# A gated delta-rule recurrence on one core: the first leaf in pieces, a gram split over two waits, reciprocals by way of DRAM, queries moved on GpSimd

## The chip, the cores and the metric

The kernel runs on one core of a Trainium2 chip. The metric is the device time of one execution in microseconds; three runs of the kernel before took 3096.86, 3099.18 and 3108.70 us, median 3099.18. Engines: TensorE (PE), VectorE (DVE), ScalarE (ACT), GpSimd (POOL), and SyncE (SP), which issues the DMAs.

## The reference

One block over x of 2048 tokens and 256 channels: x plus an attention layer, then a feed-forward layer with 8 experts. The change touches the attention's recurrence and its output norm (and a semaphore of the projections). Per head (16 heads of 128):

```python
def step(S, t):
    y = einsum('bhvk,bhk->bhv', S, k_t)
    err = y - v_t
    S = a_t[..., None] * S - (b_t[..., None] * err)[..., None] * k_t[:, :, None, :]
    o = einsum('bhvk,bhk->bhv', S, q_t)
...
mu = mean(o); var = mean(square(o - mu))
o = (o - mu) * rsqrt(var + LN_EPS) * ln_g + ln_b
g = sigmoid(x @ Wg)
return (o * g) @ Wo
```

## The kernel before

Three stages run one after the other: project_inputs (q, k, v, decays a, gates g, all stored to DRAM in scr), recurrence, and feed_forward. All is float32.

The recurrence goes over 32 chunks of 64 tokens (C). A chunk is cut into 16 leaves of 4 tokens (J = 16, R = 4), and all 16 heads are handled together. In a chunk the carried state ST is first applied to the keys and queries of the whole chunk: four "contact" matmul groups of four heads (L1558), each into one PSUM bank, which ACT copies into PQ (contact_copy, L1244). Then come the leaves in order. For leaf j, DVE multiplies the leaf's coefficients in NC by the leaf's right-hand side (L1137), adds up (L1140) to the solution W, and multiplies it by a decay (L1147) into WR, WT or WE. TensorE transposes that (L1723), ACT copies it to WL, TensorE merges it with the masked products of keys ("grams", in BD or OWN) into psM, and leaf j+1 reads psM. A merge after leaf j spans 1, 2, 4 or 8 leaves (merge_of). The gram of the eight-leaf merge after leaf 7 fills two banks, grams 2 and 3 (L1590), masked by ACT (mask_gram_act, L1355), both in the chunk that uses them: after the contacts on TensorE; ahead of leaf 0's WL copy and at leaf 2 on ACT.

At the chunk's end (behind leaf 15) ACT gathers W's last leaves in WE, TensorE transposes WE (L1767), ACT copies that to WTOK, TensorE forms the updates of the state (L1665), DVE adds them (L1087), and the next chunk's contacts follow. GpSimd computes block decays (L816), scales parts of PQ and WT, makes the decayed W (decayed_w, L838 to L843), the decayed queries of the chunk before (decayed_q, into FQ, which is the same memory as SQ) and the output gates (L860).

The output of chunk g-1 is finished inside chunk g, spread over its leaves: squares (ACT, leaf 9), variances (TensorE "var", leaf 10), square root (ACT deviation, L1392, leaf 12), a transpose (TensorE "dev", L1616), a reciprocal on DVE (invert, L1065, leaf 13), eight transposes that broadcast it ("rstd", L1621, leaf 14) and DVE's norm from PSUM (L1070, leaf 15, ahead of the additions to the state). In odd chunks from 3 on the projection by Wo runs too (wo, L1628 and L1688), so that odd and even chunks differ.

The order is written out by hand, leaf by leaf, for every engine (short_jobs and leaf_jobs for TensorE, the chunk functions of the others). Each engine works its own queue in order, with semaphore waits between. TensorE's results go through a ring of five PSUM banks, which a placement computed ahead of time gives out, the longest-held first.

## Time and profile before

| what | value |
|---|---|
| median of three runs | 3099.18 us (3096.86 to 3108.70) |
| span of the profiled execution | 3102.6 us |
| PE / DVE / ACT / POOL busy over the span | 88% / 72% / 52% / 44% |
| projections | 0 to about 620 us |
| recurrence, 32 chunks | about 620 to 2760 us |
| feed-forward | about 2760 us to the end |

The profile is one execution, its span 3.4 us longer than the median. Busy shares tell little for the recurrence, where engines take turns; it is read from the timeline, in which a bracket at the end of a row gives the idle time before it and who ended it.

### The profile page before, as it was taken

What the parts mean: (1) busy time and instruction counts of PE and PEld (TensorE: products, weight loads), DVE (VectorE), ACT (ScalarE), POOL (GpSimd) and SP (SyncE); (2) the same over time, 40 slices, a digit from 0 to 9 for tenths busy, and PEclk for the clock granted to TensorE, in tenths of its full rate; (3) what the DMA queues carried; (4) which work ended last, traced back from release to release, by engine and by line L of the source; (5) the groups of instructions that cost most, each with busy time, mean ns of one, the idle gap of its engine ahead of it and who ended that gap; (6) DMA issues with size and microseconds to landing.
All of it is one profiled execution on the core that took longest, in us unless ns stands there. A gap on an engine that the chain in (4) does not pass through costs nothing. (4 is left out here: it accounts for less than half of the span.)

```text
span 3102.6 us, 48417 instructions
## 1 busy us (share of the span) xinstructions
PE 2732.2 (88%) x14144; PEld 1863.5 (60%) x14144; DVE 2239.8 (72%) x4680; ACT 1610.3 (52%) x3516; POOL 1377.8 (44%) x1760
## 2 busy tenths in 40 slices
PE   7999999768898888988889888898888888859999
PEld 3555555446666666666666666666666666635555
DVE  6777777677888878888788887888887888623332
ACT  6666666545555555555555555555555555412111
POOL 3666676734544445444454444544445444310000
PEclk9999999989999999999999999999999999979999
DMA  3655556533232232322323223232223222034120
GB/s 124 241 225 206 233 230 239 196 82 67 43 57 42 44 65 47 57 42 43 64 49 57 42 44 59 53 57 42 44 51 61 46 53 43 9 107 109 45 38 14
DMA packets 449883, 261.22 MB, mean 84 GB/s; under 512 B 402672, under 2 KB 414672, under 8 KB 447472
## 3 DMA queue, kind: packets, MB, share of 16 engines
q1 hardware_dynamic: 449664, 258.51, 31.5%
q8 instruction: 112, 1.84, 0.3%
q14 instruction: 107, 0.88, 0.1%
HBM read 153.42 MB, written 105.05 MB: 83 GB/s over the span
## 5 line engine op out<-in xcount | busy, mean ns | idle before, releaser
L265 DVE SCALAR_TENSOR_TENSOR A_acc<-A_psY,A_w,A_acc 128x410 f32<-128x410 f32 (+1 forms) x720 | 419.2, 637 | 151.6 <-ACT A_acc L334 151.6
L405 PE MATMUL A_psY<-A_xT,A_w 128*128 128x413 f32 (+1 forms) x960 | 347.2, 510 | 9.1 <-PE A_psAG L411 7.7
L1244 ACT ACTIVATE B_PQ<-B_psM 128x64 f32<-128x64 f32 (+2 forms) x480 | 125.2, 261 | 441.2 <-DVE B_NC L1137 440.9
L1137 DVE TENSOR_TENSOR B_NC<-B_NC,B_psM 128x256 f32<-128x256 f32 x480 | 200.8, 418 | 182.5 <-PE B_psM L1756 92.8
L192 POOL TENSOR_TENSOR A_outs<-A_outs,A_acc 128x410 f32<-128x410 f32 (+1 forms) x240 | 229.7, 987 | 216.1 <-ACT A_outs L342 216.1
L899 POOL TENSOR_TENSOR B_WT<-B_WT,B_G 128x128 f32<-128x128 f32 (+2 forms) x224 | 143.4, 640 | 371.2 <-ACT B_WT L1244 184.3
L1244 ACT ACTIVATE B_WL<-B_psT 64x128 f32<-64x128 f32 (+3 forms) x480 | 148.5, 309 | 265.6 <-PE B_psT L1723 265.4
L405 PEld LDWEIGHTS A_psY<-A_xT,A_w 128*128 128x128 f32 x960 | 180.2, 189 | 165.5 <-issue 164.2
L1140 DVE TENSOR_REDUCE B_W<-B_NC 128x64 f32<-128x320 f32 x512 | 248.7, 486 | 17.6
L334 ACT ACTIVATE A_acc<-A_psY,A_w 128x410 f32<-128x410 f32 (+1 forms) x240 | 166.1, 692 | 162.9 <-PE A_psY L405 161.2
L879 POOL TENSOR_TENSOR B_PQ<-B_PQ,B_G 128x256 f32<-128x256 f32 x128 | 89.4, 699 | 345.5 <-DVE B_WT L1105 345.5
L1756 PE MATMUL B_psM<-B_BD,B_WL 128*128 128x128 f32 x1536 | 228.2, 288 | 12.4 <-ACT B_WL L1244 4.6
L1756 PEld LDWEIGHTS B_psM<-B_BD,B_WL 128*128 128x128 f32 x1536 | 192.5, 192 | 71.9 <-ACT B_WL L1244 69.5
L411 PE MATMUL A_psAG<-A_xT,A_w 128*128 128x410 f32 (+1 forms) x640 | 233.1, 506 | 0.0
L887 POOL TENSOR_TENSOR B_PQ<-B_PQ,B_G 128x256 f32<-128x256 f32 (+1 forms) x192 | 159.6, 845 | 128.3 <-DVE B_WE L1147 127.6
L1023 DVE TENSOR_TENSOR B_NC<-B_NC,B_TMP 128x384 f32<-128x384 f32 (+1 forms) x192 | 184.7, 962 | 3.3
L411 PEld LDWEIGHTS A_psAG<-A_xT,A_w 128*128 128x128 f32 x640 | 120.9, 189 | 99.6 <-issue 99.6
L1568 PE MATMUL B_ring<-B_KQ,B_KL 128*128 128x256 f32 x512 | 139.5, 396 | 25.4 <-DMA B_KQ<-scr 25.3
L1733 PE MATMUL B_psM<-B_OWN,B_WL 64*128 64x128 f32 x448 | 106.7, 319 | 51.7 <-ACT B_WL L1244 51.7
L2048 ACT ACTIVATE C_act_g<-C_psG 128x512 f32<-128x512 f32 (+1 forms) x56 | 33.4, 597 | 228.3 <-PE C_psU L2103 228.3
L1723 PE MATMUL B_psT<-ident,B_WR 128*64 128x128 f32 x256 | 75.7, 296 | 86.3 <-DVE B_WR L1147 85.1
L850 POOL TENSOR_TENSOR B_SQ<-B_PQ,B_E 128x256 f32<-128x256 f32 x128 | 129.4, 1012 | 47.0 <-DVE B_WT L1147 45.6
(207 smaller groups left out, 6588.4 us busy)
## 6 DMA issues: line engine op xcount, KB each, us to landing
B_KQ<-scr SPq DMA_DIRECT2D x96, 512.0 KB, 6.6
scr<-A_outs SPq DMA_DIRECT2D x48, 615.0 KB, 3.5
scr<-A_outag SPq DMA_DIRECT2D x32, 615.0 KB, 5.2
scr<-A_outs SPq DMA_DIRECT2D x48, 409.0 KB, 2.5
A_xc<-nbeta SPq DMA_DIRECT2D x16, 1024.0 KB, 5.9
B_A<-scr SPq DMA_DIRECT2D x32, 512.0 KB, 4.6
B_C<-scr SPq DMA_DIRECT2D x32, 512.0 KB, 6.3
B_G<-scr SPq DMA_DIRECT2D x32, 512.0 KB, 4.6
```

The costliest lines, as they stand in the source:

```text
L192: nc.gpsimd.tensor_tensor(o, o, acc[:, p, n % 2, 0:t1 - t0], ALU.mult).then_inc(silu[p].sem, 1)
L265: nc.vector.scalar_tensor_tensor(a, y, w[:, s, col:col + 1], a, ALU.mult, ALU.add)\
L334: nc.scalar.activation(acc[:, p, n % 2, 0:t1 - t0], psY[p][:, y0:y0 + t1 - t0], ACT.Identity, scale=w[:, s, col + HALO:col + HALO + 1], bi ...
L405: last = nc.tensor.matmul(psY[p][:, y0:y0 + HALO + t1 - t0], wp[:, p, kt, :], xT[:, kt, t0:t1 + HALO], start=kt == 0, stop=kt == KT - 1)
L411: last = nc.tensor.matmul(psAG[p][:, 0:t1 - t0], wp[:, A_ + p, kt, :], xT[:, kt, HALO + t0:HALO + t1], start=kt == 0, stop=kt == KT - 1)
L887: tt(x, x, gl.to_broadcast([128, H, n]), ALU.mult).then_inc(psc.sem, 1)
L899: tt(dst, dst, gr, ALU.mult).then_inc(wsc.sem, 1)
L1023: tt(out, in0, in1, op).then_inc(ncs.sem, 1)
L1137: tt(eq[:, :, :, 1:5], eq[:, :, :, 1:5], left.unsqueeze(2).to_broadcast([128, H, R, R]), ALU.mult)\
L1140: nc.vector.tensor_reduce(W[:, :, lf], eq, AXIS.X, ALU.add).then_inc(ws.sem, 1)
L1244: copy = lambda out, in_: nc.scalar.activation(out, in_, ACT.Copy)
L1756: last = mm(psM[:, 512 * q + rs * i:512 * q + rs * (i + 1)], WL[0:rs, 128 * i:128 * (i + 1)], BD[0:rs, bank, col + rs * part:col + rs * (p ...
```

## The change

- First leaf: DVE multiplies the coefficients by each contact bank straight from PSUM, four heads at a time, and adds up in two halves (first_leaf). ACT's contact copy of a bank waits for DVE's piece of that bank. Later waits on leaf_terms and w_solved are shifted by the added counts.
- Gram 3 of the next chunk is computed at the end of the chunk, one matmul group behind the WE transposes and one behind the updates (next_gram); ACT masks it behind its copy of W's rows. Gram 2 stays behind the contacts, and its mask goes behind leaf 0's WL copy.
- Norm: no dev and rstd transposes. DVE takes the reciprocal in place of the square roots (8 partitions of 128), SyncE stores it to DRAM (rstd_d) and loads it back broadcast to all partitions into FQ, which is SQ; DVE's norm reads that. The square root moves from behind leaf 12 to ahead of leaf 11's WL copy.
- Leaf 15: DVE writes its decayed W straight into WE; ACT's last gather covers leaves 12 to 14.
- GpSimd: decayed_q parts 0 to 2 go later, and wait for the norm of the chunk before instead of the square root; scale_left of leaf 1 goes ahead of them.
- Projections: one semaphore w_used with three counts takes the place of three.

The diff, cut to its core:

```diff
-        -1: [("gram", 2), ("gram", 3)],
+        -1: [("gram", 2)],
...
-        12: ([("gram", 0)] if not last else []) + ([("dev", 0)] if out else []) + ([("wo_rest", 0)] if wo else []),
+        12: ([("gram", 0)] if not last else []) + ([("wo_rest", 0)] if wo else []),
...
-        14: [("ktok", 1)] + ([("rstd", 0)] if out else []) + ([("wo_rest", 1)] if wo else []) + ([("rstd", 1)] if out else []),
+        14: [("ktok", 1)] + ([("wo_rest", 1)] if wo else []),
...
+            def spread_rstd(o):
+
+                wait(sp, rd, o, 1)
+                wait(sp, rld, o, 0)
+                sp.dma_start(rstd_d, sdev[:]).then_inc(rst.sem, 16)
+                wait(sp, rst, o, 1)
+                sp.dma_start(FQ, rstd_d.rearrange("i x -> (i x)").partition_broadcast(128)).then_inc(rld.sem, 16)
...
                 scale_right(g, 1)
                 scale_right(g, 3)
+                past(g, 1)
+                scale_left(g, 1)
                 if g:
                     decayed_q(g - 1, 0)
-                scale_left(g, 1)
-                past(g, 1)
-                if g:
-                    decayed_q(g - 1, 1)
                 past(g, 2)
...
             def invert(o):
-                ps = take_bank(dve, o + 1, "dev", 0)
-                nc.vector.reciprocal(rdev[:], ps[:, 0:8]).then_inc(rd.sem, 1)
+                wait(dve, sd, o, 1)
+                nc.vector.reciprocal(sdev[:], sdev[:]).then_inc(rd.sem, 1)
 
             def norm(o, i):
-                ps = take_bank(dve, o + 1, "rstd", i)
+                wait(dve, rld, o, 1)
                 x = O[:, 8 * i:8 * (i + 1), :]
-                tt(x, x, ps[:].rearrange("p (h c) -> p h c", h=8), ALU.mult).then_inc(on.sem, 1)
+                tt(x, x, SQ[:, 8 * i:8 * (i + 1), :], ALU.mult).then_inc(on.sem, 1)
...
+            def first_leaf(g, eq):
+
+                for n in range(4):
+                    h = slice(4 * n, 4 * n + 4)
+                    left = take_bank(dve, g, "contact", n)[:].rearrange("p (h q t) -> p h q t", h=4, q=2)[:, :, at_p(g), 0:R]
+                    tt(eq[:, h, :, 1:5], eq[:, h, :, 1:5], left.unsqueeze(2).to_broadcast([128, 4, R, R]), ALU.mult)\
+                        .then_inc(ap.sem, 1)
+                    if n == 1:
+                        wait(dve, awm, g - 1, 3)
+                        wait(dve, wxc, g - 1, 1)
+                    if n % 2:
+                        half = slice(8 * (n // 2), 8 * (n // 2) + 8)
+                        wait(dve, ap, g, n + 1)
+                        nc.vector.tensor_reduce(W[:, half, 0:R], eq[:, half], AXIS.X, ALU.add).then_inc(ws.sem, 1)
...
                 for i in range(4):
                     ps = take_bank(act, g, "contact", i)
+                    wait(act, ap, g, i + 1)
...
-                wait(act, wt, g, J)
+                wait(act, wt, g, JM)
                 wait(act, wsc, g, JM // 2)
                 wait(act, wsc0, g, JM // 2 + 1)
-                copy(w_end(12, J), w_leaves(12, J)).then_inc(wec.sem, 1)
+                copy(w_end(12, JM), w_leaves(12, JM)).then_inc(wec.sem, 1)
...
                 w_rows_copy(g)
+                if more:
+                    wait(act, mps, g, 16)
+                    mask_gram_act(g + 1, 3)
...
                     if i % 4 == 3:
                         last.then_inc(wtp.sem, 1)
+                next_gram(g, 0)
                 for i in range(4):
                     run_job(g, ("update", i))
+                next_gram(g, 1)
```

What that does to the queues, in three places. TensorE, from leaf 14 of an odd chunk over its end to the next chunk's leaf 0 (L1595 key tokens, L1621 rstd, L1688 projection, L1767 transposes of WE, L1665 updates, L1558 contacts, L1590 grams 2 and 3), before:

```order
L1595 MATMUL B_ring<-ident,B_KQ 128x128 x4
L1621 MATMUL B_ring<-ident,B_rdev 128x128 x4
L1688 MATMUL B_ring<-B_wo,B_OG 128x256 x4
L1621 MATMUL B_ring<-ident,B_rdev 128x128 x4
L1767 MATMUL B_psM<-ident,B_WE 128x128 x8
L1665 MATMUL B_ring<-B_WTOK,B_KTOK 128x128 x16
L1558 MATMUL B_ring<-B_KQ,B_ST 128x128 x16
L1590 MATMUL B_ring<-B_KQ,B_KC 128x256 x4
L1723 MATMUL B_psT<-ident,B_WR 64x128
```

and in the changed kernel (lines 1626, 1727, 1807, 1687, 1589 and 1621 are the same steps; 1704 is the moved gram):

```order
L1626 MATMUL B_ring<-ident,B_KQ 128x128 x4
L1727 MATMUL B_ring<-B_wo,B_OG 128x256 x4
L1807 MATMUL B_psM<-ident,B_WE 128x128 x8
L1704 MATMUL B_ring<-B_KQ,B_KC 128x256
L1687 MATMUL B_ring<-B_WTOK,B_KTOK 128x128 x16
L1704 MATMUL B_ring<-B_KQ,B_KC 128x256
L1589 MATMUL B_ring<-B_KQ,B_ST 128x128 x16
L1621 MATMUL B_ring<-B_KQ,B_KC 128x256 x2
L1762 MATMUL B_psT<-ident,B_WR 64x128
```

The two rstd bundles are gone, and half of what stood behind the contacts now stands on both sides of the updates.

VectorE, from the additions to the state to the next leaf 0 (L1087 additions, L1023 last step of the leaf solutions, L1137/L1140/L1147 the leaf, L1100 scale_leaf), before:

```order
L1087 TENSOR_TENSOR B_ST<-B_ST,B_ring 128x4x128 [waits B_state_decayed,B_bank3_full]
L1023 TENSOR_TENSOR B_NC<-B_NC,B_TMP 128x128x3 [waits B_leaf_solutions]
L1137 TENSOR_TENSOR B_NC<-B_NC,B_PQ 128x16x4x4 [waits B_decayed_w,B_w_rows_copied,B_contact_copied,B_leaf_solutions]
L1140 TENSOR_REDUCE B_W<-B_NC 128x16x4 [waits B_leaf_terms]
L1147 TENSOR_TENSOR B_WR<-B_W,B_E 128x64 [waits B_w_solved]
L1100 TENSOR_TENSOR B_PQ<-B_PQ,B_E 128x32x4 [waits B_contact_copied]
L1105 TENSOR_TENSOR B_WT<-B_WR,B_E 128x64 [waits B_w_decayed]
```

and in the changed kernel (1101, 1037, then four pieces 1135 and two sums 1143, 1175, 1114):

```order
L1101 TENSOR_TENSOR B_ST<-B_ST,B_ring 128x4x128 [waits B_state_decayed,B_bank2_full]
L1037 TENSOR_TENSOR B_NC<-B_NC,B_TMP 128x128x3 [waits B_leaf_solutions]
L1135 TENSOR_TENSOR B_NC<-B_NC,B_ring 128x4x4x4 [waits B_bank4_full,B_leaf_solutions]
L1135 TENSOR_TENSOR B_NC<-B_NC,B_ring 128x4x4x4 [waits B_bank0_full]
L1143 TENSOR_REDUCE B_W<-B_NC 128x8x4 [waits B_leaf_terms,B_w_rows_copied,B_decayed_w]
L1135 TENSOR_TENSOR B_NC<-B_NC,B_ring 128x4x4x4 [waits B_bank1_full]
L1135 TENSOR_TENSOR B_NC<-B_NC,B_ring 128x4x4x4 [waits B_bank2_full]
L1143 TENSOR_REDUCE B_W<-B_NC 128x8x4 [waits B_leaf_terms]
L1175 TENSOR_TENSOR B_WR<-B_W,B_E 128x64 [waits B_w_solved]
L1114 TENSOR_TENSOR B_PQ<-B_PQ,B_E 128x32x4 [waits B_contact_copied]
L1119 TENSOR_TENSOR B_WT<-B_WR,B_E 128x64 [waits B_w_decayed]
```

The leaf's product no longer waits for the contact copies but for the banks; L1114 still waits for the copies.

VectorE from leaf 13's decay product over the reciprocal and four steps of the leaf solutions to leaf 14's product, before:

```order
L1147 TENSOR_TENSOR B_WT<-B_W,B_E 128x64 [waits B_w_solved]
L1065 RECIPROCAL B_rdev<-B_ring 128x8 [waits B_bank4_full]
L1023 TENSOR_TENSOR B_NC<-B_NC,B_TMP 128x128x3 [waits B_leaf_solutions]
L1023 TENSOR_TENSOR B_NC<-B_X,B_NC 128x128
L1023 TENSOR_TENSOR B_TMP<-B_X,B_NC 128x512 [waits B_leaf_solutions]
L1023 TENSOR_TENSOR B_NC<-B_NC,B_TMP 128x128x2x2 [waits B_leaf_solutions]
L1137 TENSOR_TENSOR B_NC<-B_NC,B_psM 128x16x4x4 [waits B_merge_ps]
```

and in the changed kernel (1175, 1079, 1037, 1162 are the same steps):

```order
L1175 TENSOR_TENSOR B_WT<-B_W,B_E 128x64 [waits B_w_solved]
L1079 RECIPROCAL B_E<-B_E 8x128 [waits B_sdev]
L1037 TENSOR_TENSOR B_NC<-B_NC,B_TMP 128x128x3 [waits B_leaf_solutions]
L1037 TENSOR_TENSOR B_NC<-B_X,B_NC 128x128
L1037 TENSOR_TENSOR B_TMP<-B_X,B_NC 128x512 [waits B_leaf_solutions]
L1037 TENSOR_TENSOR B_NC<-B_NC,B_TMP 128x128x2x2 [waits B_leaf_solutions]
L1162 TENSOR_TENSOR B_NC<-B_NC,B_psM 128x16x4x4 [waits B_merge_ps]
```

The reciprocal keeps its place, reads SBUF instead of a bank, and has 128 elements on 8 partitions instead of 8 on 128.

## Rows read from the trace of the kernel before

**Rows 1.** Busy time of the engines by stage: us, then each engine, clock, DMA.

```profile
900.00:2850.00 1950.00, 1694.50 (x10337) 1241.11 (x10337) 1500.95 (x3310) 1038.80 (x2417) 860.78 (x1162) 0.98 0.27 53
```

**Rows 2.** Timeline of SyncE: start us, us it took to issue; loads of K, KB, Q.

```profile
763.82 4.39 SPq L719 DMA_DIRECT2D B_KQ<-scr  x3
...
1865.27 4.09 SPq L719 DMA_DIRECT2D B_KQ<-scr  x3
...
1994.33 4.54 SPq L719 DMA_DIRECT2D B_KQ<-scr  x3
...
2582.96 4.26 SPq L719 DMA_DIRECT2D B_KQ<-scr  x3
```

**Rows 3.** Timeline, all engines, end of an even chunk and the next leaf 0.

```profile
1864.95 0.27 DVE L1147 TENSOR_TENSOR B_WT<-B_W,B_E 128x64 f32<-128x64 f32 x1
...
1865.82 1.06 PE L1767 MATMUL B_psM<-ident,B_WE 128*128 128x128 f32 x8 [0.62 <-ACT B_WE L1244]
1866.34 1.27 DVE L1070 TENSOR_TENSOR B_O<-B_O,B_ring 128x512 f32<-128x512 f32 x2
...
1866.64 0.40 POOL L816 TENSOR_TENSOR B_G<-B_E 128x128 f32<-128x128 f32 x1 [3.16 <-issue]
...
1868.49 2.48 DVE L1087 TENSOR_TENSOR B_ST<-B_ST,B_ring 128x512 f32<-128x512 f32 x4 [0.88 <-PE B_ring L1665]
...
1873.19 0.84 POOL L843 TENSOR_TENSOR B_WX<-B_A,B_WX 128x256 f32<-128x256 f32 x1
...
1873.72 0.60 ACT L1244 ACTIVATE B_PQ<-B_ring 128x512 f32<-128x512 f32 x1 [0.29 <-PE B_ring L1558]
...
1874.41 0.42 DVE L1137 TENSOR_TENSOR B_NC<-B_NC,B_PQ 128x256 f32<-128x256 f32 x1 [2.65 <-ACT B_PQ L1244]
...
1875.58 0.28 DVE L1100 TENSOR_TENSOR B_PQ<-B_PQ,B_E 128x128 f32<-128x128 f32 x1
```

**Rows 4.** Timeline, TensorE, end of an odd chunk.

```profile
1669.67 1.89 PE L1688 MATMUL B_ring<-B_wo,B_OG 128*128 128x256 f32 x8
...
1671.84 1.04 PE L1767 MATMUL B_psM<-ident,B_WE 128*128 128x128 f32 x8
```

**Rows 5.** Leaf 13 to 14 in the timeline; reciprocals: count, ns min/median/max.

```profile
1664.77 0.42 DVE L1137 TENSOR_TENSOR B_NC<-B_NC,B_psM 128x256 f32<-128x256 f32 x1 [0.16 <-PE B_psM L1756]
...
1859.16 0.71 PE L1756 MATMUL B_psM<-B_BD,B_WL 128*128 128x128 f32 x4
...
1860.97 0.42 DVE L1137 TENSOR_TENSOR B_NC<-B_NC,B_psM 128x256 f32<-128x256 f32 x1
...
L1065 DVE RECIPROCAL B_rdev<-B_ring x32: 198/200/207, 756.9 to 2738.1; 128x8 f32<-128x8 f32 x32
...
L223 DVE RECIPROCAL A_std<-A_std x4: 177/178/178, 14.0 to 26.5; 128x4 f32<-128x4 f32 x4
```

**Rows 6.** A VectorE product beside a busy GpSimd; all products of that line.

```profile
1706.38 1.16 POOL L899 TENSOR_TENSOR B_WT<-B_WT,B_G 128x512 f32<-128x512 f32 x1 [5.76 <-ACT B_WT L1244]
1706.54 1.47 DVE L1023 TENSOR_TENSOR B_TMP<-B_X,B_NC 128x384 f32<-128x384 f32 x1
...
L1023 DVE TENSOR_TENSOR B_TMP<-B_X,B_NC x108: 589/684/1479, 926.9 to 2643.7; 128x512 f32<-128x512 f32 x54, 128x384 f32<-128x384 f32 x54
```

**Rows 7.** Windows of one us: engines as in Rows 1, then TensorE's granted clock.

```profile
1730.00:1731.00 1.00, 0.00 (x0) 0.00 (x0) 0.93 (x4) 0.22 (x1) 0.00 (x0) 1.00 0.00 0
...
1732.00:1733.00 1.00, 0.95 (x3) 0.76 (x4) 1.00 (x2) 0.00 (x0) 0.46 (x1) 0.50 0.00 0
```

**Rows 8.** DMA issues: KB each, median us from issue to landing.

```profile
A_xc<-nbeta SPq DMA_DIRECT2D x16, 1024.0 KB, 5.9
...
att<-B_att SPq DMA_DIRECT2D x16, 128.0 KB, 1.7
```

**Rows 9.** Timeline behind the last chunk: last square root, first norm.

```profile
2737.36 0.36 ACT L1392 ACTIVATE B_E<-B_ring,B_eps 8x128 f32<-8x128 f32 x1 [2.95 <-PE B_ring L1612]
...
2739.62 0.69 DVE L1070 TENSOR_TENSOR B_O<-B_O,B_ring 128x512 f32<-128x512 f32 x1 [1.27 <-PE B_ring L1621]
```

More of the change, by code:

```diff
@@ L458, in chunk_jobs @@
     if g < 0:
-        return [("own", 0, 0), ("own", 0, 1), ("kk", 0, 0), ("kk", 0, 1), ("gram", 0)]
+        return [("own", 0, 0), ("own", 0, 1), ("kk", 0, 0), ("kk", 0, 1), ("gram", 0), ("gram", 3)]
     if g == NCH:
-        return [("qk", n, l) for n in range(3) for l in range(2)] + [("oc", 0), ("oc", 1), ("var", 0), ("dev", 0), ("rstd", 0), ("rstd", 1)]
+        return [("qk", n, l) for n in range(3) for l in range(2)] + [("oc", 0), ("oc", 1), ("var", 0)]
     if g > NCH:
@@ L466, in chunk_jobs, with last_chunk @@
         jobs += [job for job in short_jobs(g, j) + leaf_jobs(g, j) if job[0] not in ("oc_rest", "wo_rest")]
-    return jobs + [("update", i) for i in range(4)]
+    return jobs + [("update", i) for i in range(4)] + ([("gram", 3)] if not last_chunk(g) else [])
+def last_chunk(g):
+    return g + 1 == NCH
 JOBS = [(g, *job) for g in range(-1, NCH + 2) for job in chunk_jobs(g)]
@@ L757, in _ @@
                 loaded(sp, what, NCH - 1)
+            wait(sp, rst, NCH, 0)
+            wait(sp, rld, NCH, 0)
             wait(sp, ldc, NCH, 0)
@@ L1613, in shared_job @@
                                   start=i == 0, stop=i == 7)
-                elif kind == "dev":
-                    wait(pe, sd, g - 1, 1)
-                    last = nc.tensor.transpose(ps[:, 0:8], sdev[:], ident[0:8, 0:8])
-                elif kind == "rstd":
-                    wait(pe, rd, g - 1, 1)
-                    for m in range(4):
-                        i = 4 * n + m
-                        last = nc.tensor.transpose(ps[:, 128 * m:128 * (m + 1)],
-                                                   rdev[:, i:i + 1].to_broadcast([128, 128]), ident[:])
                 elif kind == "wo":
@@ L1667, in updates, with next_gram @@
                             last.then_inc(filled, 1)
+            def next_gram(g, part):
+                if g + 1 == NCH:
+                    return
+                ps, filled = open_bank(pe, g, "gram", 3) if part == 0 else (ring[place[g, "gram", 3][0]], full[place[g, "gram", 3][0]])
+                if part == 0:
+                    loaded(pe, "KB", g + 1)
+                    loaded(pe, "Q", g + 1)
+                    wait(pe, kc, g + 1, 2)
+                (j, i), (bank, col) = [item for item in grams.items() if item[1][0] == 3][part]
+                p, w_, r0 = merge_of(j)
+                hp = 128 // w_
+                left = KC[:].rearrange("p n c -> p (n c)")[:, 256 + 128 * i:][:, 0:128]
+                last = mm(ps[:, col:col + 256], left, KQ[:, (g + 1) % 2, 1:3, i * hp:(i + 1) * hp, r0:r0 + w_], start=True, stop=True)
+                if part:
+                    last.then_inc(filled, 1)
             def run_job(g, job):
```

99 lines of the change are left out of this document (50 added, 49 removed).

## The prediction

> **What bounds the kernel now.** I read the windows by stage first. In the recurrence no engine is full: of 1950 us TensorE (PE) is busy 1694, VectorE (DVE) 1501, ScalarE (ACT) 1039 and GpSimd (POOL) 861 [rows 1]. So it is a chain between engines, and what counts is what ends last at each hand-over. Next, the loads of SyncE show the period, since the load of K, KB and Q goes out once a chunk: an undisturbed pair of chunks takes 1994.33 - 1865.27 = 129.06 us, and the mean pair (2582.96 - 763.82) / 14 = 129.94 [rows 2]. The 0.9 us between the two belong to TensorE's clock, below. There are 15.5 such pairs, so 1 us a pair is 15.5 us, which is just 0.5% of the kernel, about what a measurement of it can tell from no change. Last, I read the timeline where one chunk ends and the next begins, and around leaf 13.
>
> **The change, part by part.** Let 0 be the start of leaf 15's decay product (L1147) at 1864.95.
>
> *The end of a chunk, even chunks* [rows 3]. TensorE's eight transposes (L1767) start at 1865.82, and the row names what they waited for: ACT's copy into WE. That copy waited for L1147. Now DVE writes leaf 15 into WE itself and ACT's copy covers leaves 12 to 14 only, so it stands right behind the copy of key tokens; I take 0.3 us off, not the whole 0.5 that DVE's write alone would allow. The first half of the moved gram lies between the transposes and the updates. A gram bank is four matmuls, about 1 us for two halves, and the halves meet two waits that are each nearly as long; I charge 0.05. So the additions to the state (L1087) and with them the contact banks come 0.25 us earlier. DVE's idle 0.88 us ahead of L1087 covers that.
>
> *The end of a chunk, odd chunks* [rows 4]. Here TensorE is the late one: the key tokens, one rstd bundle, the projection L1688 at 1669.67, another rstd bundle, and L1767 at 1671.84 with no wait. Both bundles go, about 0.4 us each after overlap: -0.8, +0.05 for the gram half, say -0.7.
>
> *The first leaf* [rows 3]. Before, DVE starts at 1874.41, behind the last of ACT's four contact copies (1873.72, 0.60 long). Now DVE takes each contact bank as it fills. A piece of 64 elements costs about 0.21 (the rows' 0.42 for 256 and 0.28 for 128 fall by about 0.14 per 128). Behind the last piece ACT still copies its bank, and scale_leaf (L1100) waits for it: 1873.72 + 0.21 + 0.60 + hand-overs = 1874.63 against 1875.58 now, 0.95 earlier. That is the most this part can give, if nothing else holds L1100 or L1147. The mask of gram 2 goes behind the WL copy, where ACT has room; gram 3's mask falls into ACT's wait for the first contact bank.
>
> *What may hold them.* The norms (L1070 at 1866.34, two of 0.68) read PSUM today. After the change both of their inputs lie in SBUF. The trace shows what such a product does beside a busy GpSimd: at 1706.54 one took 1.47 us where its least is 0.59, and it got going when the GpSimd product of 1706.38 ended [rows 6]. The same hold works the other way round. GpSimd's block_decays start at 1866.64, 0.3 us behind the first norm, and its products end at 1874.03 (1873.19 + 0.84). If the norms push that back by their remaining 0.9 us, the last one ends at 1874.9, at 1875.1 with L1147 between. L1147 and L1100 at the first leaf read SBUF twice as well, and would want the port at 1874.1 to 1874.4. Then L1100 starts at about 1875.0, not 1874.4 (1874.63 less the 0.25). By this an even chunk gains 0.6 in all instead of 1.2, an odd one about 0.8 instead of 1.6: 1.4 us a pair with the hold and 2.8 without it. I take 1.4, since [rows 6] is the same kind of product.
>
> The Trainium skill has a rule on this (SBUF — State Buffer, section "SBUF: two separate sides"): the port pair that VectorE and GpSimd share is "an exclusive lock", held for a whole instruction, by a VectorE product with two SBUF inputs too. By that rule the gain is the 1.4; without it, it would be 2.8; the trace agrees with the rule at 1706.54.
>
> *Reciprocals at leaf 13.* A reciprocal of 4 elements a partition takes 0.178 us and one of 8 takes 0.200 [rows 5]. The new one has 128. Products grow by 0.14 us from 128 to 256 elements, 1.1 ns an element [rows 3]; at that rate it would take 0.33. The slope between its own two rows (0.022 / 4 = 5.5 ns an element) gives 0.20 + 120 x 0.0055 = 0.86. These rows are the same instruction, so I take 0.86, i.e. 0.66 more, and keep 0.13 more as the other end. None of it is covered in an even chunk: leaf 14's product starts at 1860.97 without idle time, while the matmul that it needs had begun at 1859.16 and took 0.71. In an odd chunk the same product waited 0.16 for TensorE (1664.77), which covers as much now that the dev transpose is gone from its queue. Cost: 2 x 0.66 - 0.16 = 1.2 us a pair (0.1 at the other end).
>
> The Trainium skill says that the pipe divides with "a repeat count of 8" (VectorE: DVE Perf Modes, section "First, the fixed hardware budget"). Taken as eight cycles an element that would be an estimate of 1.2 us for the instruction, and 0.7 us a pair more than I charge, 3117 in all; no row here has so many elements.
>
> *The way through DRAM.* After the reciprocal, SyncE writes 4 KB, waits, and issues a broadcast of 512 KB. A store lands in 1.7 us; the nearest broadcast is 1024 KB in 5.9 [rows 8], so half of it I put at 4.3. Leaf 13's decay product ends at about 1858.4, the reciprocal at 1859.3, the store lands at 1861.2, the broadcast at about 1866, against a norm that wants it at 1866.34 + 0.66 = 1867.0. It is hidden by 1 us in even chunks and by more in odd ones. On SyncE only the att store and the next K, KB, Q load queue behind it, and they wait for leaf 15 anyway. At the end of the recurrence nothing hides it: from the square root (2737.36, 0.36) to the first norm it was 2739.62 [rows 9]; now 1 + 2 + 4.3 = about 7.3 behind 2737.7: 5 us once.
>
> *The rest.* GpSimd's later queries keep their number and lie before anyone asks for them; the deviation's earlier place on ACT is one where ACT waits for transposes; one semaphore for three in the projections removes no work. Nothing.
>
> *TensorE's clock.* At 1730 to 1731 TensorE does nothing, and from 1732 its granted clock is 0.50, the lower of its two levels, 1.2 GHz instead of 2.4 [rows 7]. This gap between leaf 13's and leaf 14's work is in every even chunk, and the longer reciprocal widens it from 1.5 to 2.2 us; where the rstd bundles stood, TensorE now idles another 1.2 us. Falls cost 0.9 us a pair today. I put them at 1.2 after (+0.3); the bounds are 0 and +1.4 (a fall in every even chunk, at the chunk's end where TensorE is on the chain).
>
> *Sum per pair:* -1.4 + 1.2 + 0.3 = +0.1 us, times 15.5 = +1.6; with the end +5: about +7. The span goes from 3102.6 to 3109.5, and as the profiled span lies 3.4 us above the median of 3099.2, I predict **3106 us**.
>
> **The rivals.** (1) *One of the two prices is not paid.* If the reciprocal runs at one element a cycle, or if the hold on the port does not reach the first leaf, 1.1 or 1.4 us a pair come back: 3106 - 20 = 3086, on the edge of what counts as faster. For it: two rows with 4 and 8 elements, 0.02 us apart, are little to draw a slope from, and the hold depends on tenths of a microsecond. (2) *Neither is paid:* 3106 - 15.5 x 2.5 = 3067. (3) *The clock (slower).* If the widened gap takes the clock down in every even chunk, the transposes, the gram half and the updates run at 1.2 GHz on the chain: +1.1 us a pair above my 0.3: 3106 + 17 = 3123. It decides when two falls in three chunks become the rule. For it: no work fills the gap; against: today most even chunks pass with 1.5 us. (4) *The broadcast is late (slower).* If it lands over 7.7 us after the reciprocal in even chunks, both norms and the state's additions behind them on DVE wait; 1.5 us late costs, less the cover of 0.9, 0.6 us in an even chunk and nothing in an odd one, +9: 3115; with KQ's load in its way twice that. That the gram's new place does nothing is no rival: without it TensorE would still be busy when the first leaf's transpose comes.
>
> **How the numbers follow.** Forecast 0.33; (1) 0.22, half of it past the line at 3083.7; (2) 0.17; (3) 0.18; (4) 0.10. Faster by over 0.5%: 0.11 + 0.17 = 0.28. Slower by over 0.5% (above 3114.7): 0.28. Within: 0.33 + 0.11 = 0.44. The likeliest case's own range is 3098 to 3114. The range of 3062 to 3132 takes in (2) and (3).
>
> **What would show it.** A reciprocal row near 0.9 us (or 0.3); L1147 and L1100 of leaf 0 longer than 0.27 and 0.29; GpSimd's last product ending near 1874.9 on this scale; L1767 0.3 and 0.7 us behind where I put it or not; the norm waiting for a DMA or not; the mean pair at 130.0 and the count of clock falls. The forecast is wrong if DVE is not what starts leaf 14, or if a ring bank or a load turns up as a new wait.

## The result, and the profile after

The changed kernel takes **3112.31 us** (median of 6 runs, 3106.33 to 3115.26) against 3098.75 (6 runs) for the kernel before: a ratio of 1.0038, 95% interval 1.0024 to 1.0052. It is slower by a small amount that this measurement can just see, and within the half per cent that the prediction called no change. The profiled execution has a span of 3112.4 us, 9.8 more than that of before.

The period hardly moved. The loads of K, KB and Q in the timeline of SyncE (start us, us it took to issue):

```profile
759.24 4.27 SPq L720 DMA_DIRECT2D B_KQ<-scr  x3
...
1733.48 4.02 SPq L720 DMA_DIRECT2D B_KQ<-scr  x3
...
1863.18 4.32 SPq L720 DMA_DIRECT2D B_KQ<-scr  x3
...
2581.79 5.57 SPq L720 DMA_DIRECT2D B_KQ<-scr  x3
```

The mean pair is (2581.79 - 759.24) / 14 = 130.18 us (129.94 before [rows 2], forecast 130.0); the pair between the second row and the third is 129.70. Under this calm lie large moves. First the same product, leaf 13, leaf 14 and then leaf 0 of an even chunk, and leaf 15 and leaf 0 around an odd chunk's end, in the timeline of the kernel **before**:

```profile
1858.14 0.27 DVE L1147 TENSOR_TENSOR B_WT<-B_W,B_E 128x64 f32<-128x64 f32 x1
...
1861.94 0.27 DVE L1147 TENSOR_TENSOR B_WR<-B_W,B_E 128x64 f32<-128x64 f32 x1
...
1875.39 0.27 DVE L1147 TENSOR_TENSOR B_WR<-B_W,B_E 128x64 f32<-128x64 f32 x1
...
1930.07 0.27 DVE L1147 TENSOR_TENSOR B_WT<-B_W,B_E 128x64 f32<-128x64 f32 x1
...
1941.48 0.27 DVE L1147 TENSOR_TENSOR B_WR<-B_W,B_E 128x64 f32<-128x64 f32 x1
```

Its leaf 15 in the even chunk is at 1864.95 [rows 3], so leaf 15 to the next leaf 0 took 10.44 us there, 11.41 in the odd one, and leaf 13 to 14 3.80. (L1147 is L1175 now, L1767 is L1807, L1100 is L1114, L1070 is L1084.) **After**, an even chunk's end, all engines:

```profile
1855.38 0.27 DVE L1175 TENSOR_TENSOR B_WT<-B_W,B_E 128x64 f32<-128x64 f32 x1
...
1859.86 0.27 DVE L1175 TENSOR_TENSOR B_WR<-B_W,B_E 128x64 f32<-128x64 f32 x1
...
1862.86 0.27 DVE L1175 TENSOR_TENSOR B_WE<-B_W,B_E 128x64 f32<-128x64 f32 x1
...
1863.61 1.67 PE L1807 MATMUL B_psM<-ident,B_WE 128*128 128x128 f32 x8 [1.37 <-ACT B_WE L1272]
...
1866.07 2.64 PE L1687 MATMUL B_ring<-B_WTOK,B_KTOK 64*128 64x128 f32 x32
...
1869.23 3.81 PE L1589 MATMUL B_ring<-B_KQ,B_ST 128*128 128x128 f32 x32
...
1873.69 0.27 DVE L1175 TENSOR_TENSOR B_WR<-B_W,B_E 128x64 f32<-128x64 f32 x1
```

Leaf 13 to 14 is 4.48; leaf 15 to leaf 0 is 10.83, longer than before. The way from the first contact matmul (L1589) to leaf 0's product is 4.46, where it was 5.51; but from the transposes (L1807) to L1589 it is 5.62, where it was 4.06 (before, the contact matmuls start at 1869.88). The eight transposes take 1.67 us (1.06 in rows 3). The windows say why (engines as in rows 1, then the granted clock):

```profile
1858.00:1860.00 2.00, 0.43 (x4) 0.19 (x2) 1.90 (x5) 0.22 (x1) 0.00 (x0) 1.00 0.60 215
...
1864.00:1865.00 1.00, 1.00 (x7) 1.00 (x6) 1.00 (x3) 0.53 (x1) 0.45 (x1) 0.50 0.37 87
```

Between 1858 and 1860 TensorE has 0.43 us of work, later it stands 1.37 us before L1807, and while the eight transposes run, the granted clock goes to 0.50, 1.2 GHz. It was below 0.9 over this stretch at all 14 ends of the even chunks 2 to 28 (the first chunk is 0), against 5 of 14 before. An **odd** chunk's end has full clock:

```profile
1928.90 0.27 DVE L1175 TENSOR_TENSOR B_WE<-B_W,B_E 128x64 f32<-128x64 f32 x1
...
1929.89 1.04 PE L1807 MATMUL B_psM<-ident,B_WE 128*128 128x128 f32 x8
...
1933.93 3.81 PE L1589 MATMUL B_ring<-B_KQ,B_ST 128*128 128x128 f32 x32
...
1938.38 0.27 DVE L1175 TENSOR_TENSOR B_WR<-B_W,B_E 128x64 f32<-128x64 f32 x1
1938.46 0.91 POOL L857 TENSOR_TENSOR B_WX<-B_A,B_WX 128x256 f32<-128x256 f32 x1
...
1938.72 0.80 DVE L1114 TENSOR_TENSOR B_PQ<-B_PQ,B_E 128x128 f32<-128x128 f32 x1
...
1941.55 0.27 DVE L1175 TENSOR_TENSOR B_WT<-B_W,B_E 128x64 f32<-128x64 f32 x1
```

Leaf 15 to leaf 0 is 9.48 us, 1.93 less. At leaf 0 the scaling L1114 takes 0.80 us instead of 0.29: it ends right behind GpSimd's L857, at 1939.37. It reads 0.79 or 0.80 behind 14 of 14 odd chunks and 0.29 behind every even one, and leaf 0 to leaf 1 is 3.17 instead of 2.54. The pieces L1135, one of whose inputs is in PSUM, keep their 0.22 us beside GpSimd's products.

The reciprocal (count, ns min/median/max), the broadcast (KB, us from issue to landing), and the end of the recurrence:

```profile
L1079 DVE RECIPROCAL B_E<-B_E x32: 933/933/941, 751.6 to 2736.4; 8x128 f32<-8x128 f32 x32
```

```profile
B_SQ<-rstd SPq DMA_DIRECT2D x32, 512.0 KB, 3.5
```

```profile
2735.97 0.36 ACT L1421 ACTIVATE B_E<-B_ring,B_eps 8x128 f32<-8x128 f32 x1 [2.82 <-PE B_ring L1643]
2736.36 0.94 DVE L1079 RECIPROCAL B_E<-B_E 8x128 f32<-8x128 f32 x1 [16.30 <-ACT B_E L1421]
2737.32 0.29 SPq L736 DMA_DIRECT2D rstd<-B_E  x1
2738.54 0.34 SPq L738 DMA_DIRECT2D B_SQ<-rstd  x1
2741.96 1.29 DVE L1084 TENSOR_TENSOR B_O<-B_O,B_SQ 128x512 f32<-128x512 f32 x2 [4.67 <-DMA B_SQ<-rstd]
```

From the last square root to the first norm it is 5.99 us, for 2.26 before [rows 9].

**Where the 9.8 us are.** I cut the two spans at the same places: leaf 15 of the first chunk, leaf 15 of the last chunk but one, and the last store of the attention output.

| stretch | before | after | difference |
|---|---|---|---|
| start to leaf 15 of chunk 0 | 697.76 | 694.17 | -3.6 |
| 30 chunks | 1947.96 | 1948.86 | +0.9 |
| last chunk and output | 109.14 | 114.02 | +4.9 |
| last store to the end of the span (feed-forward) | 347.74 | 355.35 | +7.6 |

The first row says nothing of the change: leaf 15 of chunk 0 comes at 693.3 to 698.9 in the fourteen profiles of this study, with the changed grams at 694.2 in one kernel and at 698.3 in another. The last row is code that the change does not touch. In the fourteen profiles it takes 347.7 to 355.4 us, and one kernel, profiled twice, gave 348.3 and 351.1. So most of the difference between the two profiled spans is no effect of an edit, or at least none that is shown.

### The profile page after: what moved, and what is told of

It reads as the page before. It is cut to its first block and busy times, and to the rows that moved or that the text cites. A ratio compares the mean times of both kernels' runs of the same rounds, so it can differ in the third digit from the quotient of the medians.

```text
span 3112.4 us, 48158 instructions
## 1 busy us (share of the span) xinstructions
PE 2729.2 (88%) x13856; PEld 1849.1 (59%) x13856; DVE 2288.6 (74%) x4808; ACT 1611.5 (52%) x3516; POOL 1392.2 (45%) x1760
## 5 line engine op out<-in xcount | busy, mean ns | idle before, releaser
L1165 DVE TENSOR_REDUCE B_W<-B_NC 128x64 f32<-128x320 f32 x480 | 233.2, 486 | 16.5
```

Of the source, the lines that this page charges most:

```text
L1165: nc.vector.tensor_reduce(W[:, :, lf], eq, AXIS.X, ALU.add).then_inc(ws.sem, 1)
```

## The experiments

All ratios are to the kernel before, run beside it on the same chip (medians of 3096.9 to 3099.1 us). The table counts the even chunk ends at which TensorE's granted clock was below 0.9 while the last transposes and the first updates ran, and gives the mean pair in the profiled execution by leaf 15 of chunks 1 and 29 (before 129.78, after 130.06 by this measure). Both come from one execution of each kernel. The mean granted clock of the whole program is on record for every execution and points the same way: 0.974 to 0.981 for the kernel before, 0.961 to 0.964 for the changed one, 0.961 to 0.963 for norm_only, 0.969 to 0.972 for short_recip and filler2, 0.974 to 0.978 for filler3, 0.978 to 0.982 for bank_order in its two runs, and 0.982 to 0.984 for bank_filler.

| kernel | median us | ratio, 95% | ends at half clock | mean pair |
|---|---|---|---|---|
| old_norm | 3095.23 | 0.9989 (0.9976 to 1.0003) | 0 of 14 | 129.51 |
| norm_only | 3134.54 | 1.0119 (1.0103 to 1.0136) | 14 | 132.01 |
| filler | 3101.67 | 1.0013 (1.0001 to 1.0024) | 4 | 129.72 |
| short_recip | 3074.05 | 0.9924 (0.9907 to 0.9940) | 12 | 128.30 |
| bank_order | 3063.96 | 0.9888 (0.9871 to 0.9904) | 5 | 127.59 |
| first_only | 3100.15 | 1.0004 (0.9994 to 1.0014) | 1 | 129.62 |
| gram_only | 3129.49 | 1.0093 (1.0076 to 1.0110) | 8 | 131.40 |
| filler2 | 3100.29 | 1.0007 (0.9994 to 1.0020) | 12 | 129.70 |
| filler3 | 3087.12 | 0.9960 (0.9948 to 0.9972) | 7 | 128.66 |
| bank_early_q | 3065.35 | 0.9885 (0.9865 to 0.9904) | 4 | 127.39 |
| bank_filler | 3060.60 | 0.9873 (0.9855 to 0.9892) | 0 | 127.08 |
| bank_order_again | 3062.95 | 0.9882 (0.9864 to 0.9901) | 5 | 127.42 |

### old_norm: the change without its new normalization

```diff
-        14: [("ktok", 1)] + ([("wo_rest", 1)] if wo else []),
+        14: [("ktok", 1)] + ([("rstd", 0)] if out else []) + ([("wo_rest", 1)] if wo else []) + ([("rstd", 1)] if out else []),
...
-                nc.vector.reciprocal(sdev[:], sdev[:]).then_inc(rd.sem, 1)
+                ps = take_bank(dve, o + 1, "dev", 0)
+                nc.vector.reciprocal(rdev[:], ps[:, 0:8]).then_inc(rd.sem, 1)
...
-            spread_rstd(NCH - 1)
```

> The changed kernel with the normalization path of the kernel before: deviation after leaf 12, one transpose of the deviations at leaf 12, a reciprocal of 128x8, eight broadcasting transposes at leaf 14, no store and no broadcast through DRAM; pieces at the first leaf, gram split and the later queries stay. The theory (the chunk boundary gained what the trace of the changed kernel shows, and the new normalization path took it back in three parts: VectorE's longer reciprocal 0.68 and 0.42 us in an even and an odd chunk, TensorE's clock 1.57 us at the even chunk's end and 0.3 at leaf 12, and 3.4 us in the epilogue) expects leaf 13 to leaf 14 at 3.8 and 4.07 us, full clock at the even chunk's end, from the last scaling of a chunk to the first of the next 9.3 us (even) and 9.5 (odd), a pair of chunks at 126.7 where undisturbed, and some 3055 to 3065 us. The rival in which the clock falls come from the shorter boundary itself expects the reciprocal and the epilogue back alone: a pair at 128.6 and about 3090 us. The rival in which the boundary's gain is an artefact of where the time is cut expects 3098, the kernel before.

Measured 3095 us: both the theory's 3055 to 3065 and the first rival's 3090 missed. The second rival's 3098, the kernel before, is nearest, but its reason, that the boundary's gain is an artefact, is not the one: contact to leaf 0 kept its gain (4.46 us for 5.51). The reciprocal's time came back (leaf 13 to 14 at 3.80 and 4.07) and so did the clock, but an even boundary was 10.38 us, not 9.3, and an odd one 11.56. The timeline of an even end, and under it the line of the waits from 900 to 2650 us, in which 27 chunks end (us in total, times, longest):

```profile
1861.12 1.06 PE L1801 MATMUL B_psM<-ident,B_WE 128*128 128x128 f32 x8 [0.50 <-ACT B_WE L1257]
...
1863.08 0.70 PE L1698 MATMUL B_ring<-B_KQ,B_KC 128*128 128x256 f32 x2 [0.90 <-DVE B_O L1069]
...
1863.71 2.06 PE L1681 MATMUL B_ring<-B_WTOK,B_KTOK 64*128 64x128 f32 x32
...
PE B_ring L1698 <- DVE B_O L1069: 23.2, 27, 1.0
```

The moved gram (L1698) stands 0.90 us behind VectorE's normalization. That is no dependence of data. By the placement in the kernel's own code the gram's bank in the ring was that of the second half of the broadcast reciprocals, and these are read until the normalization ends. So the new normalization path does something that the diff doesn't say: it takes the one tenant out of the ring that the moved gram would have to wait for.

### norm_only: the new normalization alone, on the kernel before

```diff
-                ps = take_bank(dve, o + 1, "dev", 0)
-                nc.vector.reciprocal(rdev[:], ps[:, 0:8]).then_inc(rd.sem, 1)
+                wait(dve, sd, o, 1)
+                nc.vector.reciprocal(sdev[:], sdev[:]).then_inc(rd.sem, 1)
...
+                sp.dma_start(rstd_d, sdev[:]).then_inc(rst.sem, 16)
+                wait(sp, rst, o, 1)
+                sp.dma_start(FQ, rstd_d.rearrange("i x -> (i x)").partition_broadcast(128)).then_inc(rld.sem, 16)
```

> The kernel before with the normalization through DRAM alone (deviation at leaf 11, reciprocal of 8x128, store, broadcast, no transposes of it on TensorE). The theory expects leaf 13 to 14 at 4.5 us in both kinds of chunk (3.80 and 4.07 before), TensorE at half clock at the end of most even chunks, a pair at about 131 to 132 us (129.06 undisturbed before, plus 1.1 for the reciprocal and up to 1.9 for the clock), the epilogue 3.4 us longer, and 3125 to 3135 us in all. The rival (the clock falls come from the shorter boundary and not from the missing transposes) expects a pair at 130.2 to 130.9 with as many falls as before, and 3116 to 3119 us.

3134.54 us and a mean pair of 132.01: as the theory said. Timeline of TensorE at an even end:

```profile
1880.09 1.91 PE L1764 MATMUL B_psM<-ident,B_WE 128*128 128x128 f32 x8 [1.49 <-ACT B_WE L1251]
...
1882.03 2.76 PE L1662 MATMUL B_ring<-B_WTOK,B_KTOK 64*128 64x128 f32 x32
```

The transposes take 1.91 us for 1.06, the updates 2.76 for 2.06. With the first leaf and the grams as before, 14 of 14 even ends run at half clock: it is not the shorter boundary that lowers the clock. It is what left TensorE's queue, or the longer reciprocal; short_recip tells these two apart. (The kernel also has the single semaphore of the projections, ahead of the recurrence.)

The total holds something that the theory did not name. Behind an odd chunk the transposes come 0.87 us earlier, but contact to leaf 0 takes 6.19 us for 5.51:

```profile
1956.26 0.84 POOL L850 TENSOR_TENSOR B_WX<-B_A,B_WX 128x256 f32<-128x256 f32 x1
...
1956.29 1.10 DVE L1144 TENSOR_TENSOR B_NC<-B_NC,B_PQ 128x256 f32<-128x256 f32 x1 [2.54 <-ACT B_PQ L1251]
```

Leaf 0's product takes 1.10 us for 0.42 beside GpSimd's last product. It is the hold that the prediction priced, here on the product itself.

### short_recip: the reciprocal cut short

```diff
-                nc.vector.reciprocal(sdev[:], sdev[:]).then_inc(rd.sem, 1)
+                nc.vector.reciprocal(sdev[:, 0:8], sdev[:, 0:8]).then_inc(rd.sem, 1)
```

> The changed kernel with the reciprocal cut to the first 8 of 128 columns; the other columns stay deviations, so the normalization is left out for most rows. It prices VectorE's reciprocal alone. The theory expects leaf 13 to 14 at 3.80 and 4.07 us again, so 1.1 us less in a pair, 0.7 less in the epilogue, and about 3094 us, with TensorE still at half clock at the even chunk's end, since its work is as small as before. The rival (the longer wait of TensorE for the reciprocal is what lowers the clock) expects the clock back too: another 1.9 us in a pair, and about 3066 us.

```profile
L1079 DVE RECIPROCAL B_E<-B_E x32: 182/182/191, 750.0 to 2705.2; 8x8 f32<-8x8 f32 x32
```

182 ns for 933, and 3074.05 us: 20 under the theory's 3094 and 8 over the rival's 3066, so both missed. Leaf 13 to 14 fell to 3.78 and 3.80 us in the mean, 0.7 in both kinds of chunk and not 0.7 and 0.4: the 4.07 of the odd chunk before was not VectorE's, so my 1.1 was too small as a bound and 1.4 is what the instruction costs in the changed kernel. 12 of 14 even ends kept half clock, against the rival, which is why it isn't 3066; together with norm_only this leaves the work that left TensorE's queue as the main cause of the falls. The other 16 us of the 38 under the changed kernel lie in fewer or shorter clock falls elsewhere (mean pair 128.30, where 1.4 less gives 128.66), in the epilogue (114.02 to 110.73 us) and in the feed-forward part; I didn't separate them.

### first_only and gram_only: one half of the boundary each, on the kernel before

```diff
+                    tt(eq[:, h, :, 1:5], eq[:, h, :, 1:5], left.unsqueeze(2).to_broadcast([128, 4, R, R]), ALU.mult)\
+                        .then_inc(ap.sem, 1)
...
+                        first_leaf(g, eq)
...
```

> The kernel before with the first leaf in pieces alone: grams, normalization and the order of the queries stay. The theory expects from the first contact matmul to the first scaled W of a chunk 4.45 us for 5.51, nothing else changed, so 2.1 us less in a pair (127 undisturbed), and 3063 to 3068 us. The rival (the gain of the changed kernel's boundary needs the gram out of the way) expects less than 0.4 us per chunk and 3085 or more.

```diff
+                next_gram(g, 0)
                 for i in range(4):
                     run_job(g, ("update", i))
+                next_gram(g, 1)
...
```

> The kernel before with the eight-leaf gram split into TensorE's two waits at the chunk's end, and the last W written straight into its place; first leaf, normalization and order of the queries stay. The theory expects no gain at the first leaf (5.5 us from contact to W), and TensorE waiting about 1 us per chunk at the moved gram for the bank that the broadcast reciprocals hold until VectorE has normalized: a pair at 131 us and 3120 to 3130 us. The rival (taking the gram from behind the contact matmuls is worth something by itself, since leaf 0's second product follows sooner) expects 0.3 to 0.6 us per chunk back, and 3100 to 3115.

The pieces alone changed nothing (3100.15, forecast 3063 to 3068: a miss), though the way from contact to leaf 0's W did fall from 5.51 to 4.46. The timeline shows where it went:

```profile
1871.25 1.89 PE L1604 MATMUL B_ring<-B_KQ,B_KC 128*128 128x256 f32 x8
...
1872.06 0.27 DVE L1160 TENSOR_TENSOR B_WR<-B_W,B_E 128x64 f32<-128x64 f32 x1
...
1872.98 0.27 PE L1737 MATMUL B_psT<-ident,B_WR 128*64 128x128 f32 x1
...
1874.79 0.97 POOL L852 TENSOR_TENSOR B_SQ<-B_PQ,B_E 128x256 f32<-128x256 f32 x1
...
1875.22 0.66 DVE L1160 TENSOR_TENSOR B_WT<-B_W,B_E 128x64 f32<-128x64 f32 x1
```

Eight gram matmuls, 1.89 us, begin behind the contact matmuls at 1871.25, and leaf 0's transpose (L1737) comes 0.92 us behind its W at 1872.06; leaf 0 to leaf 1 is 3.15 for 2.54. Then leaf 1's decay product takes 0.66 us for 0.27 beside GpSimd's query product of 1874.79, and leaf 1 to 2 is 2.91 for 2.52. The gain of 1.06 is handed back in two steps within two leaves.

The gram split alone costs 0.9%, as the theory said (3129.49 us, forecast 3120 to 3130). Its waits from 900 to 2650 us have the line of old_norm again:

```profile
PE B_ring L1692 <- DVE B_O L1075: 17.9, 19, 1.1
```

So neither half pays alone as it was tried. The pieces need the gram out of the way, and the gram needs a bank that is free. What the gram split would give alone with a free bank was not run.

### bank_order: the free bank by one line

```diff
-    return jobs + [("update", i) for i in range(4)] + ([("gram", 3)] if not last_chunk(g) else [])
+    return jobs + [("update", 0), ("update", 1)] + ([("gram", 3)] if not last_chunk(g) else []) + [("update", 2), ("update", 3)]
```

This is old_norm with the banks dealt out in another order.

> The kernel with the pieces, the gram split, the later queries and the normalization of before, with one line more: in the list that deals out the five banks of the ring, the moved gram stands between the second and the third update and not behind the fourth, so its bank is the one that the key tokens held and not the one of the second half of the broadcast reciprocals. In the trace with that list unchanged TensorE stands 0.9 to 1.0 us at the moved gram behind VectorE's normalization, in every chunk, which makes the way from the chunk's last transposes to the first update 2.6 us for 1.5. The theory (that wait is the whole reason why the old normalization gained nothing) expects 1.5 us there, a pair of chunks at 127.1 us, and 3052 to 3062 us. The rival in which the wait comes back at the next bank (the second updates, which now hold the reciprocals' banks) expects 0.5 us of it at each chunk and 3070; the rival in which TensorE's clock falls at the even chunk's end, as in the changed kernel, expects another 1.6 us per pair and 3080.

> The kernel with pieces, split gram in the key tokens' bank, the old normalization and later queries once more, beside the three above, for its interval and for the change from chip to chip. The theory expects 3060 to 3066 us and a ratio of 0.987 to 0.991; were the gain of the first run chance, the ratio would be above 0.993.

3063.96 us, 2 us above the theory's 3052 to 3062, and 3062.95 in the second run, inside its range: **1.2% faster than the kernel before**, 1.6% faster than the changed one. The wait line at the moved gram is gone, transposes to first update are 1.5 us at full clock, and the rival's wait at the second updates isn't there. The changed kernel frees the same bank, and pays for it with a store, a broadcast, a longer reciprocal and the clock.

### bank_early_q: do the later queries matter?

```diff
-                past(g, 1)
-                scale_left(g, 1)
                 if g:
                     decayed_q(g - 1, 0)
+                scale_left(g, 1)
+                past(g, 1)
...
```

> The kernel with pieces, split gram in the key tokens' bank and the old normalization, and now GpSimd's three query products in the order of before. In the run with the pieces alone VectorE's scaling at leaf 1 took 0.66 us for 0.27, with a query product of GpSimd running beside it, and the way from leaf 1 to leaf 2 was 2.91 us for 2.52. The theory (the later queries pay only through this) expects 2.52 to 2.91 us there, thus 0 to 0.8 us more per pair, and 3064 to 3076 us. The rival (GpSimd's order matters for what waits for the queries, and the early order was better) expects 3055 to 3062.

3065.35 us, no difference from bank_order, and leaf 1 to 2 at 2.52 us. So the early queries alone do not slow the decay product of leaf 1; in first_only a late leaf 1 came with them, and whether that alone is enough no run shows. The later queries are worth nothing here.

### filler, filler2, filler3, bank_filler: idle work for TensorE

```diff
+FILL = {11: (("gram", 0), 8), 13: (("decay", 2), 8), 14: (("ktok", 1), 8)}
...
+                    if g % 2 == 0 and g + 1 < NCH and j in FILL:
+                        ps = open_bank(pe, g, *FILL[j][0])[0]
+                        for m in range(FILL[j][1]):
+                            nc.tensor.transpose(ps[:, 128 * (m % 4):128 * (m % 4 + 1)], ident[:], ident[:])
```

> The changed kernel with idle work for TensorE in even chunks: eight transposes of the identity more at each of leaves 11, 13 and 14, into the bank that the next job opens, where the trace shows TensorE waiting for VectorE; nothing is computed with them. If missing work on TensorE is what lowers its clock at the even chunk's end, the clock stays at full there, the boundary of an even chunk comes to 9.3 us (10.83 in the changed kernel), leaf 12 to 13 to 2.96, a pair to 127.7 to 128.0 and the kernel to about 3083 us. If the clock falls for another reason, or the transposes stand in the way, it stays at 3112 or rises by up to 1.8 us per pair, to 3140.

Mean pair 129.72, not 128: a miss, and the trace of ScalarE and TensorE tells why:

```profile
1473.32 0.60 ACT L1273 ACTIVATE B_KTOK<-B_ring 128x512 f32<-128x512 f32 x1 [1.65 <-PE B_ring L1627]
...
1473.81 0.35 ACT L1273 ACTIVATE B_WE<-B_WT 128x192 f32<-128x192 f32 x1
...
1474.42 1.07 PE L1812 MATMUL B_psM<-ident,B_WE 128*128 128x128 f32 x8 [1.14 <-ACT B_WE L1273]
```

Idle work ahead of the key tokens made their copy late (1473.32), ScalarE's copy into WE stands behind it, and the transposes come 2.08 us behind leaf 15 in the mean of the 14 even ends for 0.84. The time, 3101.67 us, misses 3083 too. The clock was kept at 10 of 14 ends, and the time spent on the way. filler2 drops the entry for leaf 14:

> The changed kernel with eight idle transposes at each of leaves 11 and 13 of the even chunks, and none at leaf 14, where in the run with three such places the key tokens came 1.2 us later and ScalarE's copy of the last W terms stood behind their copy (last scaling to last transposes 2.13 us for 0.85). The theory expects that delay gone (0.75), and the clock at full at leaf 12 and in most chunk ends, since the idle time just ahead of the first fall and of the second is filled: a pair at 128 us and about 3083 us. The rival (the idle time at leaf 14 alone is enough to lower the clock at the chunk's end) expects full clock at leaf 12 alone, 0.3 us less in a pair than in the changed kernel, and 3105.

Mean pair 129.70, 12 of 14 ends at half clock; leaf 12 to 13 fell from 3.18 to 2.96 in the mean. The rival holds: with leaves 11 and 13 filled, idle time at leaf 14 is still enough. The time of 3100.29 is near the rival's 3105. filler3 keeps leaves 11 and 13 and puts eight transposes behind the key tokens:

```diff
+                if g % 2 == 0 and g + 1 < NCH:
+                    ps = open_bank(pe, g, "update", 0)[0]
+                    for m in range(8):
+                        nc.tensor.transpose(ps[:, 128 * (m % 4):128 * (m % 4 + 1)], ident[:], ident[:])
```

> The changed kernel with idle transposes of TensorE in even chunks: eight at leaf 11, eight at leaf 13, and eight behind the key tokens of leaf 14, into the bank that the first update opens next, so that nothing on ScalarE comes later. The run with idle work at leaves 11 and 13 alone left the fall at the chunk's end; the run with idle work ahead of the key tokens took most of it away and delayed the last transposes by 1.3 us. The theory (the fall at the even chunk's end follows from TensorE's idle time at leaf 14 and its wait there) expects the last transposes 0.75 us behind the last scaling, 1.5 us from there to the first update and 4.05 to the first contact matmul, 9.3 us for the boundary (10.95 in the changed kernel), a pair at 128.2 and about 3080 to 3088 us. If the clock still falls there, the time stays within 5 us of the run with two places, 3100.

3087.12 us: work that computes nothing makes the changed kernel 0.8% faster, and faster than the kernel before. An even end that kept its clock:

```profile
1853.41 1.04 PE L1809 MATMUL B_ring<-ident 128*128 128x128 f32 x8
...
1854.20 0.27 DVE L1176 TENSOR_TENSOR B_WE<-B_W,B_E 128x64 f32<-128x64 f32 x1
...
1854.95 1.06 PE L1816 MATMUL B_psM<-ident,B_WE 128*128 128x128 f32 x8 [0.50 <-ACT B_WE L1273]
...
1856.46 2.06 PE L1688 MATMUL B_ring<-B_WTOK,B_KTOK 64*128 64x128 f32 x32
...
1863.47 0.52 DVE L1176 TENSOR_TENSOR B_WR<-B_W,B_E 128x64 f32<-128x64 f32 x1
```

Leaf 15 to leaf 0 is 9.27 us, for 10.83. Half of the ends still fall, so it isn't all that could be had. The last row is worth a look: with TensorE at full speed the even chunk reaches leaf 0 early enough to meet GpSimd's last product (1863.02, 0.85 long), and the decay product takes 0.52 us for 0.27.

> The kernel with pieces, split gram in the key tokens' bank, the old normalization and later queries, plus eight idle transposes at leaves 11 and 13 of even chunks. Its trace without them shows half clock at the end of some even chunks (last transposes to first update 1.86 us in the mean for 1.5, to the first contact matmul 4.42 for 4.05). If idle time at these leaves lowers the clock, the mean pair comes from 127.6 to 127.1 us and the kernel to about 3056 us; if not, it stays at 3064, and if the idle work is in the way, it rises to 3070.

```profile
1838.46 0.27 DVE L1161 TENSOR_TENSOR B_WE<-B_W,B_E 128x64 f32<-128x64 f32 x1
...
1839.21 1.06 PE L1806 MATMUL B_psM<-ident,B_WE 128*128 128x128 f32 x8 [0.50 <-ACT B_WE L1258]
...
1840.11 0.60 PE L1699 MATMUL B_ring<-B_KQ,B_KC 128*128 128x256 f32 x2
...
1840.72 2.06 PE L1682 MATMUL B_ring<-B_WTOK,B_KTOK 64*128 64x128 f32 x32
...
1847.73 0.27 DVE L1161 TENSOR_TENSOR B_WR<-B_W,B_E 128x64 f32<-128x64 f32 x1
```

3060.60 us for the 3056 expected, none of the 14 even ends at half clock, mean pair 127.08 where 127.1 was expected. The price of the clock is gone from these ends. Against bank_order it is 3 us, which the intervals do not tell apart; the profile does, and the mean granted clock of the four executions (0.982 to 0.984 for 0.978 to 0.982).

## Why the prediction was right, and where it wasn't

The time came out at 3112.3 for 3106, within half a per cent of before as forecast; the working held only in part: two terms were off by about 1 us a pair, in opposite directions, so that the time hits is in good part luck. Per pair of chunks, typical pairs at full clock:

| term | forecast | measured | from |
|---|---|---|---|
| transposes L1807 earlier, even / odd | -0.3 / -0.7 | -0.12 / -0.87 | 0.87 to 0.75; 1.86 to 0.99 behind leaf 15 |
| first leaf in pieces, a chunk | -0.95 | -1.06 | 5.51 to 4.45 from contact |
| leaf 0 to 1, even / odd | (hold) | +0.12 / +0.63 | 2.54 to 2.66 / 3.17 |
| chunk's end, sum | -1.4 | -2.4 | -1.06 even, -1.30 odd |
| reciprocal | +1.2 | +1.1 | 0.68 even, 0.42 odd |
| clock | +0.3 | +1.5 | the rest of 130.18 - 129.94; L1807 to L1589 alone: mean 5.71 for 4.30 in even chunks |
| sum | +0.1 | +0.24 | |

- **The chunk's end.** The step that failed is the price of the hold between VectorE and GpSimd at leaf 0. I took 1.4 us a pair for it; it is 0.5, in the odd chunk alone. The mechanism is there (L1114 at 0.80 ends with L857), and it is the rule of the Trainium skill that the prediction cited (SBUF — State Buffer, section "SBUF: two separate sides"), which the trace agrees with. The norms push GpSimd's products back too, by less than the 0.9 us that I took: behind even chunks the last of them ends 9.10 us behind leaf 15 in the kernel before and 9.64 in the changed one; over the study it is 9.08 to 9.12 wherever the norms read PSUM and 9.62 to 9.67 wherever they read SBUF. The larger error was whom that meets. In the even chunk the slow clock makes leaf 0 so late, at 10.83, that GpSimd is through. filler3, where the clock is back at half of the ends, shows the hold there too, at 0.25 us in the row shown and at 0.24 to 0.52 in 5 of 14 ends. In bank_order, with leaf 0 at the same 9.27 us behind leaf 15 but with norms from PSUM, it is absent.
- **The reciprocal.** 933 ns, forecast 860 from the slope between two short rows; the slope from 8 to 128 elements is (933 - 182) / 120 = 6.3 ns. 0.16 us of cover in the odd chunk was 0.26. Right. The estimate of 1.2 us that I worked out from the Trainium skill (VectorE: DVE Perf Modes, section "First, the fixed hardware budget") was 0.3 us too long; no row here shows eight cycles an element.
- **The clock.** The step that failed is the choice of +0.3 between bounds of 0 and +1.4, argued with "today most even chunks pass with 1.5 us". Rival (3) named the mechanism, the place and its deciding point; two falls in three chunks was passed, it is every one. The total of (3), 3123, was too high mainly since the chunk's end gained a microsecond more than I allowed. The row that should have weighed more is that the rstd transposes stood in just the gap whose neighbours I had seen fall. norm_only (14 of 14) rules out the shorter boundary, short_recip (12 of 14) the longer reciprocal as the main cause, and filler2 against filler3 (12 and 7) shows that the place behind the key tokens of leaf 14 counts. Which of the nine transposes that went (eight rstd, one dev) counts was not separated.
- **The way through DRAM.** Landing in 3.5 us, forecast 4.3; at the end of the recurrence 5.99 us for 2.26, so +3.7 for my +5. In the chunks no norm waits for it. Right in kind; rival (4) fell.
- **The start** of the recurrence is 3.4 us sooner in this pair of profiles (leaf 3 of chunk 0 at 651.95 for 655.38), about what the epilogue costs. It is not shown to be an effect of the change: norm_only, with the grams as before, is there at 651.02, and filler3, with the new ones, at 654.78.
- **"If a ring bank turns up as a new wait"**: it did not in the changed kernel, and I hadn't seen why. The prediction priced the transposes' removal by their time on TensorE. Their seat in the ring was worth more once the gram had moved: 1.1 us at an even and 1.2 us at an odd chunk's end between old_norm and bank_order.
- **The profiled span** fell on 3109.5 + 2.9; but 7.6 of the 9.8 us between the two spans come from the feed-forward part, whose spread from one execution to the next I had not allowed for. That the sum of the rest hits as well is partly luck. The medians lie 13.6 us apart, and the table's sum and the longer way at the end make 0.24 x 15.5 + 3.7 = 7.4; the other 6 us are not located.
